# A cross-attention layer: the feed-forward matmuls on scaled pairs of 16-bit floats in place of fp32r pairs

## The reference

```python
q = (query @ Wq + bq).reshape(b, s, N_HEADS, D_K).transpose(0, 2, 1, 3)
k = (key @ Wk + bk).reshape(...)          # the same shape and order
v = (values @ Wv + bv).reshape(...)
scores = einsum('bhqd,bhkd->bhqk', q, k) / sqrt(D_K)
scores = where(j < i, scores, NEG_INF)    # strictly causal
attn = softmax(scores, axis=-1)           # row 0 is set to zero
ctx = einsum('bhqk,bhkd->bhqd', attn, v)
x = layer_norm(query + ctx @ Wo + bo, ln1_g, ln1_b)
ffn = relu(x @ W1 + b1) @ W2 + b2
out = layer_norm(x + ffn, ln2_g, ln2_b)
```

## Time and profile before

| | us |
|---|---|
| median of 3 runs (2936.40 to 2949.02) | 2943.37 |
| the profiled execution | 2933.55 |
| its span, first to last instruction | 2931.8 |
| TensorE busy with matmuls | 2806.7 |
| VectorE busy | 1857.8 |
| ScalarE busy | 1443.0 |
| GpSimd busy | 970.8 |
| attention, until about | 1262 |
| feed, until the end | 2932 |

### The profile page before, as it was taken

One profiled execution on the slowest core, in us unless ns is written; L12 is line 12 of the kernel. 1 busy time (PEld: TensorE's weight loads), 2 busy tenths in 40 slices (PEclk: granted clock), 3 DMA queues, 4 the chain that ended last, 5 costly groups with the idle time before them and its releaser, 6 DMA issues.

```text
span 2931.8 us, 64830 instructions
## 1 busy us (share of the span) xinstructions
PE 2806.7 (96%) x20300; PEld 2443.6 (83%) x20300; DVE 1857.8 (63%) x4852; ACT 1443.0 (49%) x3187; POOL 970.8 (33%) x916
## 2 busy tenths in 40 slices
PE   6999999999999999949999999999999999999998
PEld 5787878787878788738989999998989898998987
DVE  5888878887878788756455545455454555454553
ACT  4777777776777777744333333333333333332332
POOL 2666666666666666720111111110101111111100
PEclk9999999999999999979999999999999999999999
...
GB/s 153 121 134 125 130 122 132 129 130 116 131 128 131 124 124 118 97 165 73 65 44 54 53 50 57 48 52 49 58 43 57 50 51 56 50 57 44 56 43 29
DMA packets 427938, 252.99 MB, mean 86 GB/s; under 512 B 297969, under 2 KB 330673, under 8 KB 427713
## 3 DMA queue, kind: packets, MB, share of 16 engines
...
...
## 4 chain that ended last, share of the span: by engine, by line
PE 55%; DVE 1%; DMA 0%; SPq 0%; issue 0%; ACT 0%; DVEq 0%
PE h_ps L1110 25%; PE acc L1122 24%; PE front L1097 6%; DMA raw<-in_W 0%; PE front L1083 0%; SPq L704 0%; DVE W L1037 0%; DVE Wo L1037 0%; DMA x_rows<-x 0%; DVE turned L1028 0%; DVE stats L962 0%; DVE block_turned L1019 0%; DVE y L1060 0%; DVE y L974 0%; DVE x L974 0%
## 5 line engine op out<-in xcount | busy, mean ns | idle before, releaser
L358 POOL TENSOR_TENSOR prob_lo<-probs,prob_hi 128x512 f16<-128x512 f32 (+1 forms) x768 | 787.1, 1040 | 458.9 <-ACT prob_hi L420 457.1
L1110 PEld LDWEIGHTS h_ps<-turned,W 128*128 128x128 f32 x6144 | 805.5, 191 | 67.0 <-DVE turned L1028 25.5
L1110 PE MATMUL h_ps<-turned,W 128*128 128x256 f32 x6144 | 818.1, 283 | 25.1 <-DVE turned L1028 25.1
L1122 PE MATMUL acc<-W,hs 128*128 128x512 f32 x3072 | 793.2, 393 | 0.0
L951 ACT ACTIVATE hf<-h_ps,b1c 128x256 f32<-128x256 f32 x512 | 244.0, 477 | 890.1 <-PE h_ps L1110 889.4
L1069 DVE TENSOR_TENSOR hs<-hf,hs 128x256 fp32r<-128x256 f32 x512 | 230.4, 450 | 708.3 <-ACT hs L953 708.1
L1122 PEld LDWEIGHTS acc<-W,hs 128*128 128x128 f32 x3072 | 544.7, 189 | 89.5
L418 ACT ACTIVATE probs<-st_ps 128x512 f32<-128x512 f32 (+1 forms) x768 | 406.0, 529 | 289.5 <-PE st_ps L640 236.0
L513 DVE CUSTOM_DVE_ANT_0 max_ps<-max_ps,mask_q 128x256 f32<-128x256 f32 (+2 forms) x768 | 424.2, 568 | 188.4 <-PE max_ps L558 182.1
L420 ACT ACTIVATE prob_hi<-st_ps 128x512 f16<-128x512 f32 (+1 forms) x768 | 407.3, 530 | 0.0
L906 POOL TENSOR_TENSOR x<-x,vec_b 128x512 f32<-128x512 f32 x64 | 87.8, 1392 | 867.9 <-DMA x_rows<-x 867.9
...
## 6 DMA issues: line engine op xcount, KB each, us to landing
heads<-stage SPq DMA_DIRECT2D x768, 128.0 KB, 2.4
raw<-in_xT SPq DMA_DIRECT2D x64, 256.0 KB, 3.9
o_in<-ctx_rows SPq DMA_DIRECT2D x256, 64.0 KB, 2.3
...
x_rows<-x SPq DMA_DIRECT2D x64, 256.0 KB, 2.0
o_in<-x_rows SPq DMA_DIRECT2D x256, 64.0 KB, 2.4
...
raw<-in_cT SPq DMA_DIRECT2D x60, 256.0 KB, 2.9
```

The costliest lines, as they stand in the source:

```text
L358: pool.tensor_tensor(prob_lo[:, k % 4, 0:w], probs[:, k % PROBS, 0:w], prob_hi[:, k % 4, 0:w], ALU.subtract).then_inc(pl_done, 1)
L1110: last = pe.matmul(h_ps[:, f % 2, 0:T], W1[:, aw, j, f * P:(f + 1) * P], turned[:, item.parity, aa, j, :], start=(j == 0 and m == 0), stop ...
L1122: last = pe.matmul(acc[:, item.parity, u, :], hs[:, f % 4, aa, u * P:(u + 1) * P], W2[:, aw, f, :], start=(f == 0 and m == 0), stop=(f == ...
```

## The change

The feed-forward matmuls (`h_ps` and `acc`) get operands in 16-bit floats, high and low part as before, and as many matmuls of the same shapes. W1, W2, the turned `x1` and `hs` are multiplied by powers of two as they are cut, and the sums are scaled back where they are read. The projection by Wo and all of the attention's matmuls stay as they are.

The scales come from bounds: the largest magnitudes of W1, W2, b1, g1 and be1. They are found beside the attention. A new buffer `scan_chunk` of 128 x 512 floats takes one piece after another; VectorE reduces it to one maximum a partition (`look`) and joins that to the ones before (`keep`). Six pieces (b1 in four, g1, be1) are handled before the first window, one of W1 and one of W2 in each of the 16 windows, at slots 20 and 44 on VectorE, loaded by SyncE at slots 14 and 38. In the attention's last window but one the maxima of the partitions go to memory and back, and VectorE works out the scales in some twelve small operations. At the start of `feed`, VectorE waits until the attention's last stores have landed, where before it did so later (slot 5). In the diff, cut to its core, the piece at 317 is SyncE's in each slot of the attention, the one at 383 SyncE's ahead of the first window, the one at 508 VectorE's (first ahead of the windows, then in each slot, ahead of the rows of maxima), and from 885 on stands `feed`.

```diff
+    def load(self, sp, src):
+        sp.dma_start(self.chunk[:, :], src).then_inc(self.loaded, 16)
+    def look(self, dve):
+        return dve.tensor_reduce(self.part[:, :], self.chunk[:, :], AX_X, ALU.max, apply_absolute_value=True)
+    def keep(self, dve, column):
+        top = self.top[:, column:column + 1]
+        return dve.tensor_tensor(top, top, self.part[:, :], ALU.max)
...
+    SCAN = [(14, 20), (38, 44)]
...
@@ -271,6 +317,25 @@
+                    for n, (at, _) in enumerate(SCAN):
+                        for item, _ in due(window, s, SLOTS, B, at):
...
+                            wait_for_all(sp, (bounds.seen, SCANS, item, SMALL + n))
+                            bounds.load(sp, src)
+                    if isinstance(window[0], int) and (window[0], s) == (B, 2):
+                        sp.wait_ge(bounds.kept, SMALL + SCANS * B)
+                        for n in range(SCANS):
+                            sp.dma_start(bounds.rows[n:n + 1, :].rearrange("a p -> p a"), bounds.top[:, n:n + 1]
+                                         ).then_inc(bounds.spread, 16)
...
@@ -318,6 +383,10 @@
+            for n, (src, _) in enumerate(bounds.small):
+                if n:
+                    sp.wait_ge(bounds.seen, n)
+                bounds.load(sp, src)
...
@@ -439,11 +508,63 @@
+            for n, (_, column) in enumerate(bounds.small):
+                dve.wait_ge(bounds.loaded, 16 * (n + 1))
...
+                bounds.look(dve).then_inc(bounds.seen, 1)
+                dve.wait_ge(bounds.seen, n + 1)
+                bounds.keep(dve, column).then_inc(bounds.kept, 1)
...
+                    for n, (_, at) in enumerate(SCAN):
+                        for item, _ in due(window, s, SLOTS, B, at):
+                            wait_for(dve, bounds.loaded, 16 * SCANS, item, 16 * (SMALL + n + 1))
+                            wait_for(dve, bounds.kept, SCANS, item, SMALL + n)
+                            bounds.look(dve).then_inc(bounds.seen, 1)
+                            wait_for(dve, bounds.seen, SCANS, item, SMALL + n + 1)
+                            bounds.keep(dve, n).then_inc(bounds.kept, 1)
...
@@ -764,13 +885,15 @@
-        W1 = sb("W1", [P, 2, KT, FF], F32R)
-        W2 = sb("W2", [P, 2, FT, D], F32R)
+        W1 = sb("W1", [P, 2, KT, FF], F16)
+        W2 = sb("W2", [P, 2, FT, D], F16)
         turned = sb("turned", [P, 2, 2, KT, T], F32R)
+        x1_halves = sb("x1_halves", [P, 2, 2, KT, T], F16)
...
-        hs = sb("hs", [P, 4, 2, T], F32R)
+        hs = sb("hs", [P, 4, 2, T], F16)
...
                         act.activation(hs[:, f % 4, 0, :], h_ps[:, f % 2, 0:T], ACT.Relu,
-                                       bias=b1c[:, f:f + 1]).then_inc(h_out, 1)
+                                       bias=b1s[:, f:f + 1], scale=h_evac).then_inc(h_out, 1)
...
+            dve.wait_ge(bounds.ready, 1)
+            for i in range(2):
+                dve.wait_ge(early.stored[i], all_stored)
+            dve.tensor_scalar(b1s[:, :], b1c[:, :], scale_h, None, ALU.mult).then_inc(b1_scaled, 1)
...
-                            dve.tensor_tensor(y[:, u, :], acc[:, item.parity, u, :], x1[:, item.parity, u, :],
-                                              ALU.add).then_inc(y_done, 1)
+                            dve.scalar_tensor_tensor(out=y[:, u, :], in0=acc[:, item.parity, u, :], scalar=y_evac,
+                                                     in1=x1[:, item.parity, u, :], op0=ALU.mult, op1=ALU.add
+                                                     ).then_inc(y_done, 1)
...
                                 last = pe.matmul(h_ps[:, f % 2, 0:T], W1[:, aw, j, f * P:(f + 1) * P],
-                                                 turned[:, item.parity, aa, j, :], start=(j == 0 and m == 0),
+                                                 x1_halves[:, item.parity, aa, j, :], start=(j == 0 and m == 0),
```

130 lines of the change are left out of this document (115 added, 15 removed).

## The result

The changed kernel takes 2972.76 us (median of four runs, 2968.82 to 2978.23), the kernel before 2940.89 (four runs, 2936.4 to 2949.02): a ratio of 1.0107, 95% interval 1.0075 to 1.0138, so 1.1% slower. The forecast was 2975 us.

What follows compares the result with a forecast made beforehand. TensorE bounds the kernel, alone in the second half, with VectorE close behind in the first. Terms -104 + 25 + 23 + 42 + 19.5 + 20 + 6 = +31.5 us give 2975 us, 1.1% slower; range 2905 to 3055.

Steps and rivals of the forecast that it cites:

- Matmuls, -104: Feed-forward loop: 16-bit operands shorten each slot from 2.82 to 2.616 us, over 16 slots x 32 chunks: -104 us.
- Rival B: Feed-forward matmuls: 16-bit pairs stream no faster, so the gain falls away; 3054 us, chance 0.1.
- What the second half gives back, +25: Feed-forward slot 2: GpSimd's x_in work delays VectorE's norm, TensorE waits 0.85 us for hs per chunk, x 30: +25 us.
- Start, +23: Before the first window: seven serial scans ahead of the wk split make vf 22 us late, nothing hides it: +23 us.
- Slot 20, +42: Attention: late load, reduction and keep meeting GpSimd delay onorm; TensorE waits 2.8 us, 15 times: +42 us.
- Slot 44, +19.5: Attention: load lands in time, but VectorE is already waited for; the scan costs 1.3 us, 15 times: +19.5 us.
- The clock, +20: Attention: new TensorE waits bring one more stretch at clock 0.50 per item, 1.3 us each: +20 us.
- Small ones: Attention's end: last reduction and twelve scale operations, +3; second half's start: waiting for stores +2, b1s product and splits +1.
- two kinds of items: Slot 44: where L456 and L458 already lose time to GpSimd, the scan costs 0.3 us; elsewhere 1.4 to 2.5.
- Rival A: Attention: scans hidden, costing TensorE 0.8 and 0.3 us, 16.5 us for all, no clock lost; 2910 us, chance 0.22.
- Rival C: Attention: same mechanism, half the size; slot-20 loads land at 2.8 us, the clock keeps; 2940 us, chance 0.18.

Runs made afterwards that it cites:

- The two edits: Each alone against the changed kernel: x_in load issued ahead of the o_in loads, 2952.74 us; scale of h's two ACTIVATEs a constant instead of an SBUF column, 2968.82 us.
- the running maximum: Changed kernel with the keep of W1 and W2 folded into the reduction, which rewrites the maximum as a 513th column of the chunk: 2975.84 us.

## Why the prediction was right

The direction and the mechanism of every large term came out as forecast. That the sum is right to less than 1 us is luck: the median moved by 31.9 us and the sum said 31.5, but the stages of the profiled executions moved by 44.8, since the one before lies 7 us under its median (2933.55 for 2940.89) and the one after 5 us over it (2978.23 for 2972.76). By stages the second half gave back 15 us more than forecast, and the attention 6 us less.

- **Matmuls, -104.** Slot 2.61 for 2.616 us: 16 x 32 x 0.21 = -107. The `o_ps` rows carried over to matmuls of 256 and 512 columns. The figure of the Trainium skill ("TensorE: Matmul & The Clock Gate", "Wait — 56ns, not 53.3ns?") gives 215.8 ns for 512 columns and the trace 216.0. (Worked out, that figure makes the gain 110 us, not 111.) Rival B is out.
- **What the second half gives back, +25.** The wait for `hs` is 23.1 us of idle time and 28.1 counted from start to start, by the mechanism named; moving the `x_in` load took it away. But -64.3 + 107 = 43 us came back in all. The missing term is a sentence of the prediction that is wrong: the scaled ACTIVATEs do not "take their old time", and not all of it lies beside TensorE. They take 90 ns more, and cost 12 us, most of it a wait of 0.29 us for `h_ps` in each chunk's first slot, which ScalarE frees late behind two `x_halves`. The Trainium skill states this price ("ScalarE: Activation LUTs", "What ACT_TABLE_LOAD costs": about 93 ns for each operand given by a pointer); the trace agrees with 90. The two edits gave back 29.6 and 12.2 us, each alone; both together were not run.
- **Start, +23.** 23.7; `vf` at 43.91 for 42.8. Seven scans 3.7 us apart, for 3.4.
- **Slot 20, +42.** Measured 34.4, the excess of the gaps at head 14 in the fifteen items: fourteen waits of about 2.46 us, for fifteen of 2.8, since the last item's window has no scan there. The load lands sooner than forecast, after 2.5 to 2.8 us at this slot and not 3.8, and the wait for it is 1.03 us and not 1.4; but what follows is held until GpSimd's pair ends, so most of that is lost again. From the last maximum to the end of the second negation it is 2.88 us more than before, for 3.1 forecast, and the way from there to `onorm` 2.33 us, for 2.6. Mechanism right, size 20% too high, within its bounds. The share given to `keep` itself was wrong, as the running maximum shows; the sum would have been the same without it.

```profile
DMA to landing us min/median/max: 2.5/2.8/6.4
```

(All 38 loads of `scan_chunk`.)

- **Slot 44, +19.5.** 12 us, not 1.3 each. The prediction had two kinds of items and had both right: in the nine whose gap at head 6 was 2.13 us or less it grew by 1.25 in the mean, in the six where it was 2.88 to 3.00 by 0.16. The average taken over them was too high.
- **The clock, +20.** 78.8 - 34.4 - 12 - 5.8 (the exchange, below) leaves 26 us. That is a remainder and not a measurement; 65 us more at half speed (109 for 44) bound it at 32. Right in kind, about a quarter too low.
- **Small ones.** Of the last reduction and the scales I priced VectorE's operations (+3); what came is 5.8 us in the 15th item (81.9 against 76.1), by the exchange of the maxima across partitions. VectorE stands for its load, TensorE waits behind it for a maximum, and once more for the rows of maxima, whose transfers are queued behind SyncE's stand (VectorE, then TensorE):

```profile
1284.16 0.42 DVE L563 TENSOR_REDUCE scan_top<-scan_chunk 128x2 f32<-128x256 f32 x1 [2.87 <-DMA scan_chunk<-scan_rows]
...
1285.82 0.69 PE L679 MATMUL max_ps<-heads 96*128 96x384 f32 x1 [3.39 <-DVE maxima L634]
1287.87 0.80 PE L726 MATMUL st_ps<-heads 98*128 98x512 f32 x1 [1.36 <-DMA heads<-rows]
```

  The start of the second half: +6.5 for +3. VectorE's first operation there waited for the stores' landing, not their issue, and with the wait put back the way to `h_ps` is 47.0 and 45.9 us (46.5 before):

```profile
1367.68 2.90 SPq L375 DMA_DIRECT2D ctx_rows<-onorm  x1
...
1374.34 0.23 DVE L1139 TENSOR_SCALAR b1s<-b1c,scale 128x16 f32<-128x16 f32 x1 [9.82 <-DMA ctx_rows<-onorm]
```

- **Rival A** (the scans are hidden, 2910 us) did not come true, but half of its condition can be made true: with the load there before slot 20 the wait at head 14 is gone. Slot 44 still costs then (3.26 us at head 6 for 2.20), and the time is 2929 us. The 2903 us of the kernel with one item scanned are no test of it, since there are no scans to hide.
- **Rival C** (half the size, 2940 us) had its first condition fulfilled: the slot-20 loads land after 2.5 to 2.8 us. Its price for that, 15 us less, did not follow, since GpSimd's operations set the end, and the clock did not keep.

The Trainium skill's rule on the port ("SBUF — State Buffer", "SBUF: two separate sides") was used in the prediction to tell `keep` from the reduction. It covers L579 as well, which has two SBUF inputs and waits. In the trace L577, a tensor_scalar with one SBUF input, waits as `keep` does (1.17 us beside GpSimd, 0.18 without). The rule also names VectorE's fast mode on two ports; whether L577 runs in it, no run here shows. The reduction, with one input too, takes 0.69 us everywhere, as the rule would have it.
